# Bidirectional Mamba with experts on one core: eight more gates and five fewer C products on VectorE, 15 buffers for states

## What is computed

```python
x = x + attn_ref(xn, ...) + ffn_ref(xn, ...)

# attn_ref: layernorm, then a Mamba block forward and one on the reversed sequence
xi, z = split(xn @ in_w.T)                       # 256 channels each
xi = silu(conv1d(xi, taps=4) + conv_b)
dt, B, C = split(xi @ x_w.T)                     # 8, 16, 16
delta = softplus(dt @ dt_w.T + dt_b)
h = h * exp(delta * A) + (delta * xi) * B        # per step t, 16 states per channel
y = sum_n(h * C)
y = (y + xi * D) * silu(z)                       # the gate
out = y @ out_w.T                                # both directions are combined and projected

# ffn_ref: each token goes to the one of 8 experts with the largest router logit
ye = (silu(xe @ gate_w[e].T) * (xe @ up_w[e].T)) @ down_w[e].T
```

## Time and profile before

| | us |
|---|---|
| median of 3 runs | 917.0 |
| lowest, highest | 914.77, 917.44 |
| the profiled execution, its time | 917.37 |
| the profiled execution, its span | 915.4 |

### The profile page before, as it was taken

How to read it: one execution, slowest core, us unless ns; L and a number is a source line. 1 busy time by engine, 2 the same in 40 slices (tenths; PEclk the granted TensorE clock), 3 DMA queues, 4 the chain that set the end, 5 groups by cost and what they waited for, 6 DMA issues and landing times. The chain is left out here.

```text
span 915.4 us, 10734 instructions
## 1 busy us (share of the span) xinstructions
PE 741.9 (81%) x3033; PEld 331.6 (36%) x3033; DVE 881.2 (96%) x631; ACT 699.6 (76%) x1183; POOL 800.6 (87%) x450
## 2 busy tenths in 40 slices
PE   8879867877488978979887987889978877879376
PEld 5334322332034534444343534345334432324022
DVE  5999999999899999999899999999999999999896
ACT  4899956657479789888989989897979976586640
POOL 1578787999999989998898998999798999999995
PEclk9969887787798999999799999989989899879679
DMA  6795443245355556545455636455553445453300
GB/s 219 200 279 125 131 92 94 106 103 135 89 144 171 141 176 157 159 125 141 142 143 179 155 86 210 118 168 147 173 142 93 140 94 164 107 172 73 89 0 12
DMA packets 87227, 123.45 MB, mean 135 GB/s; under 512 B 7929, under 2 KB 58490, under 8 KB 83202
## 3 DMA queue, kind: packets, MB, share of 16 engines
q1 hardware_dynamic: 85122, 118.58, 46.8%
q0 software_dynamic: 2048, 4.20, 1.5%
HBM read 75.44 MB, written 14.29 MB: 98 GB/s over the span
## 5 line engine op out<-in xcount | busy, mean ns | idle before, releaser
L1368 POOL TENSOR_TENSOR hs<-hs,C_rep 128x1024 f32<-128x1024 f32 x250 | 585.3, 2360 | 47.8 <-DVE hs L1157 25.6
L954 ACT ACTIVATE dA<-delta_rep,A_sb 128x511 f32<-128x511 f32 x512 | 338.5, 717 | 98.3 <-DVE hs L1157 51.8
L1138 DVE TENSOR_TENSOR in_b<-in_b,B_rep 128x1024 f32<-128x1024 f32 x256 | 300.2, 1218 | 8.8 <-PE in_b L589 8.7
L1157 DVE TENSOR_TENSOR_SCAN hs<-dA,in_b 128x1024 f32<-128x1024 f32 x128 | 285.6, 2270 | 5.3 <-PE y L623 5.3
L1155 DVE TENSOR_TENSOR_SCAN hs<-dA,in_b 128x1024 f32<-128x1024 f32 x128 | 285.4, 2270 | 1.2 <-PE y L623 1.2
L589 PE MATMUL in_b<-du,cst 128*128 128x512 f32 x256 | 160.4, 713 | 61.4 <-DVE hs L1157 45.2
L623 PE MATMUL y<-hs,cst 128*32 128x512 f32 x1024 | 137.9, 645 | 21.8 <-POOL hs L1368 21.8
L550 PE MATMUL front<-xpad,w_in 128*128 128x512 f32 x248 | 120.0, 619 | 8.4 <-ACT xi L883 6.2
L963 ACT ACT_TABLE_LOAD x71 | 91.1, 1283 | 9.2 <-PE moe L740 5.2
L589 PEld LDWEIGHTS in_b<-du,cst 128*128 128x128 f32 x256 | 46.0, 211 | 136.4 <-issue 132.8
L550 PEld LDWEIGHTS front<-xpad,w_in 128*128 128x128 f32 x248 | 47.0, 199 | 67.2 <-issue 50.2
(11 more groups left out here) (147 smaller groups left out, 808.4 us busy)
## 6 DMA issues: line engine op xcount, KB each, us to landing
delta_rep<-tmpA SPq DMA_DIRECT2D x126, 256.0 KB, 3.9
C_rep<-dbc_scratch SPq DMA_DIRECT2D x16, 1024.0 KB, 7.3
B_rep<-dbc_scratch SPq DMA_DIRECT2D x15, 1024.0 KB, 5.2
gu_w<-in_gate_up SPq DMA_DIRECT2D x39, 384.0 KB, 3.8
dn_w<-in_down SPq DMA_DIRECT2D x39, 192.0 KB, 2.6
xs<-sorted_tokens SPq DMA_DIRECT2D x39, 64.0 KB, 3.7
sorted_ffn<-ys SPq DMA_DIRECT2D x39, 64.0 KB, 2.4
sorted_tokens<-up_f SPq DMA_DIRECT2D x9, 256.0 KB, 4.6
```

Of the source, the lines that this page charges most:

```text
L954: i = e.activation(dA[:, m % NA, r * L + 1:(r + 1) * L], src, ACT.Exp, scale=A_sb[:, d, 2 * p + jj, RH * rh + r:RH * rh + r + 1])
L1138: e.tensor_tensor(to, in_b[:, 2 + 2 * odd, :].unsqueeze(1).broadcast_to([P, RH, L]), by, ALU.mult).then_inc(dve_mult, 1)
L1157: e.tensor_tensor_scan(to[:, ::-1], a[:, 1:n + 1][:, ::-1], b[:, ::-1], 0.0, ALU.mult, ALU.add).then_inc(dve_scan, 1)
L1368: e.tensor_tensor(hs[:, m % NH, :], hs[:, m % NH, :], C_rep[:, u % 2, RH * rh:RH * rh + RH, :].rearrange("p r t -> p (r t)"), ALU.mult).th ...
```

## The change

Three constants change. `hs` gets 15 buffers in place of 13, so scan m waits for the sum that read half m - 15: scan 8b+15 for the even sum, scan 8b+16 for the odd one. Gates 2, 6, 24, 25, 26, 27, 28 and 29 go to VectorE (ScalarE loses their copies, GpSimd their multiplications). Products 41, 56, 180, 217 and 226 go from VectorE to GpSimd.

```diff
-NA, NH = 4, 13
+NA, NH = 4, 15
...
-GATE_ON_DVE = (3, 4, 5, 2 * UNITS - 1)
-C_ON_DVE = (41, 56, 180, 217, 226, LAST - 1)
+GATE_ON_DVE = (2, 3, 4, 5, 6, 24, 25, 26, 27, 28, 29, 2 * UNITS - 1)
+C_ON_DVE = (LAST - 1,)
```

## The result

| | before | after |
|---|---|---|
| median, us | 915.89 (7 runs) | 923.20 (7 runs) |
| lowest, highest | 912.40, 918.78 | 916.93, 925.66 |
| the profiled execution, its time | 917.37 | 916.93 |
| the profiled execution, its span | 915.4 | 915.1 |

The ratio of after to before is 1.0081, with a 95% interval of 1.0059 to 1.0104: the change makes the kernel **slower by 0.8%**, 7.3 us by the medians, and 923.2 lies outside the range of the prediction (912.2 to 919.8). The profiled execution is 5 us shorter than any of the other six. The same kernel ran again as e1_again, where the profiled execution took 923.49 (span 921.7). That one is near the median, and I read both. One execution of e1_again (1054.96 us) and one of the kernel before (1347.66 us) were in a slow state, and the ratios leave them out.

A forecast was written before the change was run, and what follows sets the result against it. VectorE was taken as the bound (busy 881.2 of 915.4 us), with GpSimd's backlog reaching it at two crossings. Shifts of +0.8 after the first, -0.2 before and -1.6 after the second, then gate 29, gave -1.0: 916.0 us, range 912.2 to 919.8.

The forecast's parts named there:

- Prices on VectorE: VectorE's own work: eight gates at 0.6 us add 4.8, five removed products save 7.9; it falls by 3.1 us.
- Prices on GpSimd: GpSimd's work: each added product costs 2.4 us, each removed gate frees 1.27, four long DMA issues give back 0.5 to 0.8.
- Rival 3: GpSimd's long DMA issues stay long, as the Trainium skill's page would give: 919.0 us, chance 0.10.
- First crossing: GpSimd's backlog from the scatter reaches VectorE: spread waits of 2.6 and 4.1 us at 54 and 62, shift +0.8 after gate 6.
- product 56 comes later than 54: First crossing, GpSimd at product 54: product 56 adds nothing there, so lateness is +2.2 - 0.8 = +1.4 us.
- Between the crossings: From gate 6 to gate 24: GpSimd's backlog runs out, half the lateness is absorbed, product 180 gives -1.2; shift -0.8, gate 24 -0.2.
- I take half: +0.4: Between the crossings: VectorE, 0.8 us late, waits less for spreads from a full TensorE, halving the shift to +0.4.
- Second crossing: GpSimd's backlog from the gathers reaches VectorE at block 29's even sum: GpSimd and the spread for 246 gain, shift -1.6 us.
- Rival 2: Sums after TensorE's rests run at full clock, making both crossings 1.7 us earlier: -4.4 us, 912.6 us, chance 0.19.
- 7.46 us of rest were enough for the low clock: Second crossing: argument against the full-clock rival, that TensorE's 7.46 us without work before block 29's even sum sufficed.
- Sum: Whole kernel: the shifts end at -1.0 us, set against the median of 917.0, giving 916.0 us.
- 4: GpSimd's lateness, at most 4.1 us after gate 6, reaches TensorE's expert tiles and spreads for halves 72 to 79: 920.7, chance 0.13.

The follow-up runs named there:

- e1_again: The changed kernel run once more, unaltered, for a second profile: 922.98 us, ratio 1.0085 to the kernel before.
- e3: Kernel before with only the eight gates added on VectorE (13 buffers, products as before): 919.2 us, ratio 1.0057.
- e6: The changed kernel with product 56 back on VectorE: 921.04 us, ratio 1.0069 to the kernel before.
- e7: The changed kernel with products 180, 217 and 226 back on VectorE: 923.83 us, ratio 1.0104 to the kernel before.
- e5_before: The kernel before, unchanged, run once more for a second profile: 913.82 us, ratio 0.9989.
- e13: The changed kernel with GpSimd's delta and du of the next unit put ahead of product 56: 918.95 us, ratio 1.0052 to the kernel before.
- e10: Kernel before with only 15 buffers, gates 24 to 29 on VectorE and products 180, 217, 226 on GpSimd: 919.21 us, ratio 1.0055.
- e14: The changed kernel with spreads for 62/63 and 246/247 ahead of the even sums of blocks 6 and 29: 915.67 us, ratio 1.0015 to the kernel before.
- e15: The changed kernel with e13 and e14 together, plus the spread for 54/55 ahead of block 5's even sum: 913.5 us, ratio 0.9992 to the kernel before.
- e16: Kernel before with 15 buffers and the spreads for 62/63 and 246/247 ahead of the even sums of blocks 6 and 29: 915.61 us, ratio 1.0018.
- e11: The changed kernel with unread matmuls on constants ahead of the even sums of blocks 6 and 29: 921.05 us, ratio 1.0056 to the kernel before.

## Why the prediction was wrong

The forecast was 916.0, "the same", with 0.14 on slower; it is 923.2. Its steps one by one, against e1_again:

- **Prices on VectorE**: right. -3.1 us busy, as summed; a gate takes 0.69 us and costs 0.6 in the shift (half 200 to 208: 3.00 to 3.61).
- **Prices on GpSimd**: right. 2.36 and 1.27 us, and the long issues went away with VectorE's products. They come back in e3, e6 and e7, each beside a VectorE product. In the ten traces where no such product is left but 255 no issue is over 1.19 us. The Trainium skill (SBUF — State Buffer, "Who interferes with whom") has a tensor_tensor leave descriptor writing alone, and marks the reason as inferred. The traces go the other way and decide: a product of VectorE with both inputs in SBUF does hold up the issue, here by 0.5 to 0.85 us. Rival 3 falls.
- **First crossing**: the waits at 54 and 62 came as written (2.07 and 4.38 for 2.6 and 4.1), no scan waits for a sum, and gate 6 doesn't wait. Scan 62 is at -0.4, or +0.6 counted from half 20, for +0.8. What failed is the clause "product 56 comes later than 54", with which I closed GpSimd's account. I never asked what stands behind product 56: delta of the next unit, then SP's queue, the experts' weights, TensorE and the spread for 66. Missing term: a wait of 3.2 us at half 66. The sum had nothing for it.
- **Between the crossings**: "I take half: +0.4" failed. Something was absorbed: VectorE falls from +2.9 at half 66 to +0.7 at 80, as before's wait of 1.86 us at half 78 is not there. But waits at 90, 120, 122 and 148 (5.6 us together, 2.5 at these halves before) bring it to +4.1 by half 176, or +2.9 against e5_before. e13 puts 2.3 us of it, at half 80, down to the order of delta. What stands behind the rest is not settled: e10 loses as much in that stretch without the early moves. Product 180 gave its 1.14, gate 24 took its 0.6.
- **Second crossing**: GpSimd's part is right. VectorE is at +4.2 at half 216, and the even sum starts at +2.27, so 1.9 us were won (1.4 forecast). What failed is "two matmuls of bias and residual and the spread for 246 and 247 follow it", at the old distance of 6.61 us. It was 9.35, because the low clock outlasted the sum. With the old distance the spread would have ended 2.74 us earlier and gate 29 would not have waited 0.61. Those 3.35 us are nearly the whole of the 3.7 lost there. Rival 2 had the clock as the unknown, but only as a gain: I bounded it on one side. Its "7.46 us of rest were enough for the low clock" also misread the trace, where the clock had fallen at about 851, before that rest. That the spread's place is what counts is shown by e14; the low clock's own share rests on the traces alone.
- **Sum**: counted from half 20, e1_again is at +7.3 where -1.0 was forecast, 8.3 us apart. At half 176 it is +5.1 for +0.4, 4.7 us apart. From there to 248 it loses 2.2 where 1.4 were to be won: 3.6, of which 3.35 are the second crossing's longer distance and gate 29's wait.
- **Rivals**: 4 had the mechanism, TensorE's expert tiles late by GpSimd, and 920.7 us. It came one stage earlier, by the weights' DMA at half 66 and not by products at 72 to 79, and I held it for 0.13. That its 920.7 lies nearest of all to 923.2 is in part luck, as it leaves out the second crossing. The likeliest case was too narrow: each sum, spread and DMA behind a crossing was taken at the place that it had in one trace.

## What to carry to other kernels

When a wait is removed from an in-order engine, look at the producer's queue: if the next thing needed stands behind the same late instruction, the wait only changes its name. Look at the order there before you deepen a ring. Here the order took back the loss of the change (e14, e15), but deeper ring and order together won nothing over the kernel before (e16). When an operation is put onto a late engine, list everything queued behind it up to the next point where that engine idles, and follow each one's readers through DMA queues as well; here a product that nobody was waiting for delayed one that fed an expert's weights. And where a second engine is nearly as busy as the first (here 96% and 87%), time won for one at a crossing is only kept if the other isn't behind at the end.

## What the runs showed of the hardware that I had not expected

- VectorE's product with both inputs in SBUF can stand through several GpSimd products in a row: 6.64 and 6.59 us (e3, e7), 4.77 (e16), 3.06 and 3.14 for 1.2 to 1.3 alone. In e3 and e16 it ends 1.1 us behind the last product of the row, so it wasn't let in between two of them. At product 180, where VectorE began first (652.11), it took 1.20 us and GpSimd's product 3.25 in place of 2.36. A gate, which reads PSUM, took 0.67 to 0.70 us in all traces.
- At the second crossing TensorE's granted clock was 0.50 when the sum began in the traces of both kernels, but how long it stayed there under work without a pause differed at the same place: some 3.6 us in before, some 11.5 in e1_again, and the bias matmuls show the same split between all traces with and without both late moves. Matmuls on constants ahead of the sum (e11) raised it and did not keep it up.
